# Softmax division of three attention stages: after two transposes, or on the features through DRAM

## The reference

```
x = x + SelfAttention0(layernorm(x))          # causal, 512 x 512 per head
x = x + CrossAttention0(layernorm(x), ctx)    # 64 context rows per sequence, no mask added
x = x + MixtureOfDepths(layernorm(x))         # top 128 tokens of each sequence are routed
x = x + SelfAttention1(layernorm(x))          # not causal, q and k rms-normed per head
x = x + CrossAttention1(layernorm(x), ctx, mask)
x = x + MixtureOfExperts(layernorm(x))        # 8 experts, top 2
attention = softmax(q @ k.T) @ v, heads side by side, then @ W_out
```

## Time and profile before

| | us |
|---|---|
| median of 3 runs | 2571.24 |
| lowest, highest | 2565.96, 2574.76 |
| the profiled execution, whole | 2568.06 |
| its span, first to last instruction | 2566.3 |
| self attention, causal | from about 63 to 512 |
| cross attention, routed | about 512 to 827 |
| self attention, normed | about 1070 to 1641 |

### The profile page before, as it was taken

How to read it: one execution, slowest core, us unless ns; L and a number is a source line. 1 busy time by engine, 2 the same in 40 slices (tenths; PEclk the granted TensorE clock), 3 DMA queues, 4 the chain that set the end, 5 groups by cost and what they waited for, 6 DMA issues and landing times. The chain is left out here.

```text
span 2566.3 us, 45589 instructions
## 1 busy us (share of the span) xinstructions
PE 2330.6 (91%) x14571; PEld 1519.5 (59%) x14585; DVE 1457.3 (57%) x3885; ACT 1140.1 (44%) x2685; POOL 734.6 (29%) x848
## 2 busy tenths in 40 slices
PE   7999999889996799899999999888886799999998
PEld 5455555545555566533443333445556599999997
DVE  4766676446765443577777767354545733444333
ACT  1666656523331562277777776422221033333332
POOL 3111111044421321333333221153311433333333
PEclk9999999999998999999999999999995899999999
DMA  6222222120000310322222121100009122222221
GB/s 156 88 87 90 87 76 88 31 76 5 5 1 1 105 44 1 93 63 72 66 76 68 58 73 53 40 7 9 9 1 362 57 36 33 36 36 36 36 35 22
DMA packets 135325, 148.85 MB, mean 58 GB/s; under 512 B 25286, under 2 KB 119152, under 8 KB 135024
## 3 DMA queue, kind: packets, MB, share of 16 engines
q1 hardware_dynamic: 119504, 127.23, 16.1%
q0 software_dynamic: 13680, 17.84, 4.3%
q10 hardware_dynamic: 1968, 1.60, 0.4%
HBM read 100.71 MB, written 46.01 MB: 57 GB/s over the span
## 5 line engine op out<-in xcount | busy, mean ns | idle before, releaser
L452 ACT ACTIVATE self_probs<-self_score_ps 128x512 f32<-128x512 f32 (+3 forms) x1024 | 481.0, 516 | 315.0 <-PE self_score_ps L813 162.7
L618 DVE TENSOR_REDUCE self_neg_max<-self_max_ps 128x1 f32<-128x512 f32 x512 | 328.2, 685 | 147.8 <-PE self_max_ps L799 143.3
L799 PE MATMUL self_max_ps<-self_k_stack,self_q_stack 96*128 96x512 bf16 (+3 forms) x1024 | 347.6, 342 | 21.1 <-DVE self_neg_max L615 12.3
L810 PE MATMUL self_score_ps<-self_q_stack,self_k_stack 99*128 99x512 bf16 (+3 forms) x1024 | 342.5, 342 | 1.6 <-ACT self_probs L452 1.6
L2259 ACT ACTIVATE x_stream<-experts_up_ps,experts_bias_now 128x128 f32<-128x128 f32 x568 | 162.4, 369 | 387.7 <-PE experts_up_ps L2480 387.7
L615 DVE CUSTOM_DVE_ANT_0 self_masked<-self_max_ps,self_later 128x128 f32<-128x128 f32 (+3 forms) x512 | 235.4, 488 | 124.1 <-PE self_max_ps L799 112.7
L2480 PEld LDWEIGHTS experts_up_ps<-experts_tileT,x_stream 128*128 128x128 f32 x2272 | 266.7, 193 | 5.3 <-issue 1.8
L2480 PE MATMUL experts_up_ps<-experts_tileT,x_stream 128*128 128x128 f32 x2272 | 267.2, 276 | 1.4 <-DVE x_stream L2396 1.4
L2490 PE MATMUL experts_down_ps<-experts_down,x_stream 128*128 x1136 | 256.8, 379 | 0.0
L824 PE MATMUL self_out_ps<-self_probs,self_values 128*32 128x512 f32 (+3 forms) x2048 | 231.8, 524 | 3.3 <-ACT self_probs L452 1.4
L810 PEld LDWEIGHTS self_score_ps<-self_q_stack,self_k_stack 99*128 99x128 bf16 x1024 | 98.8, 97 | 229.1 <-ACT self_probs L452 171.2
(11 more groups left out here) (293 smaller groups left out, 3962.7 us busy)
## 6 DMA issues: line engine op xcount, KB each, us to landing
self_parts_dram<-self_parts SPq DMA_DIRECT2D x64, 384.0 KB, 2.3
self_q_stack<-self_parts_dram SPq DMA_DIRECT2D x384, 64.0 KB, 2.3
self_k_stack<-self_parts_dram SPq DMA_DIRECT2D x360, 64.0 KB, 2.3
experts_up<-moe_up_dram SPq DMA_DIRECT2D x8, 1024.0 KB, 8.3
experts_down<-moe_down_dram SPq DMA_DIRECT2D x8, 1024.0 KB, 10.6
x_stream<-x_dram SPq DMA_DIRECT2D x8, 512.0 KB, 7.8
expert_rows_dram<-experts_down SPq DMA_DIRECT2D x8, 512.0 KB
out_dram<-x_stream SPq DMA_DIRECT2D x8, 512.0 KB, 8.6
```

The source lines that it names most:

```text
L452: act.activation(probs[:, i % 8, 0:w], score_ps[:, (16 * n + i) % 3, 0:w], ACT.Exp).then_inc(exp_done, 1)
L618: dve.tensor_reduce(neg_max[:, n % 2, t, h:h + 1], max_ps[:, i % 2, 0:w], AX, ALU.max, negate=True).then_inc(max_read, 1)
L799: last = pe.matmul(max_ps[:, i % 2, 0:w], q_stack[0:ROWS, h, P * t:P * t + P], k_stack[0:ROWS, h, 0:w], start=True, stop=True)
L810: last = pe.matmul(score_ps[:, m % 3, 0:w], k_stack[0:KROWS, head, P * j:P * j + P], q_stack[0:KROWS, head, S - w:S], start=True, stop=not ...
```

## The change

The division is done on features by tokens, so nothing is turned. `out_ps` is copied as before; SyncE stores `o_raw` to DRAM, and loads it back twice when a half (8 heads) of a sequence is complete: the feature rows to `o_now`, and one sum row of each head repeated 16 times to `sums`. ScalarE takes Ln of `sums` and Exp of minus that (the reciprocal); VectorE multiplies the two. Done in both self attentions and the routed cross attention. `ot`, `ob`, the copy after `ob` and the four (self: four periods') pairs of reciprocal and product go; in the self stages the last two periods of the stage keep them. In the normed self stage (`norm`) `mt` moves from chunk 0 to chunk 1 and `copy_shift` from chunk 1 to chunk 2 (`MT_STEP`). In the routed stage the loads of the next stage's weights (`router.loads()`) are issued later on SyncE, and a load of the context is issued up to three sequences ahead. The masked cross attention has the old text, in a function of its own; the routed one is a new function.

The core of the diff, self attention first:

```diff
+        out_scratch = nc.dram_tensor(f"{name}_out_dram", [2, 2 * GH, 2, HD, S], F32).ap()
+        MT_STEP = 1 if norm else 0
-            if j == 0 and n + 1 < N:
+            if j == MT_STEP and n + 1 < N:
                 work.append(("mt", n + 1))
-            if j == 1 and n >= 1:
+            if j == 1 and n == N - 1:
                 work.append(("ot", n - 1))
-                work += {(1, 1): [("ob", b - 1, 1)], (2, 0): [("e", b - 1, 0)], (2, 1): [("e", b - 1, 1)]}.get((g, j), [])
+                work += {(2, 0): [("e", b - 1, 0)], (2, 1): [("e", b - 1, 1)]}.get((g, j), [])
-            if (g, j) == (3, 1):
-                work.append(("ob", b, 0))
+                def out_store(n):
+                    b, g = n // NG, n % NG
+                    sp.wait_ge(o_copied, n + 1)
+                    wait(sp, out_loaded[g // 2], 32 * b)
+                    sp.dma_start(out_scratch[g // 2, GH * (g % 2):GH * (g % 2) + GH].rearrange("h c d t -> (h c d) t"),
+                                 o_raw[:, n % 2]).then_inc(out_stored[n % 2], 16)
+                def out_load(b, half):
+                    for i in range(2):
+                        sp.wait_ge(out_stored[i], 16 * (2 * b + half) + 16)
+                    wait(sp, o_done, 2 * (b - 1) + half + 1 if b else 0)
+                    sp.dma_start(o_now[:, half], out_scratch[half, :, 0]).then_inc(out_loaded[half], 16)
+                    sp.dma_start(sums[:, half], out_scratch[half, :, 1, 0:1].to_broadcast([2 * GH, HD, S])).then_inc(out_loaded[half], 16)
                 for b in range(B):
                     more = b + 1 < B
+                    if b >= 1:
+                        out_store(4 * b - 1)
                     place_shift(4 * b + 1)
+                    if b >= 1:
+                        out_load(b - 1, 1)
                     if more:
                         store(b + 1, 0)
                         stack(b + 1, 0)
+                    out_store(4 * b)
                     place_shift(4 * b + 2)
                     if more:
                         store(b + 1, 1)
                         stack(b + 1, 1)
+                    out_store(4 * b + 1)
                     place_shift(4 * b + 3)
+                    out_load(b, 0)
                     if more:
                         stack(b + 1, 2)
+                        out_store(4 * b + 2)
                         place_shift(4 * b + 4)
                         stack(b + 1, 3)
-                def turned_back(b, k):
+                def inverted(b, half):
+                    act.wait_ge(out_loaded[half], 32 * b + 32)
+                    act.activation(sums[:, half], sums[:, half], ACT.Ln).then_inc(sums_logged, 1)
+                    act.wait_ge(sums_logged, 2 * b + half + 1)
+                    act.activation(sums[:, half], sums[:, half], ACT.Exp, scale=-1.0).then_inc(sums_inverted, 1)
-                        if j == 1 and n + 1 < N:
+                        if j == MT_STEP + 1 and n + 1 < N:
                             copy_shift(n + 1)
                         if (g, j) == (1, 2) and b >= 1:
-                            turned_back(b - 1, 1)
+                            inverted(b - 1, 1)
-                        if (g, j) == (3, 2):
-                            turned_back(b, 0)
+                        if (g, j) == (3, 0):
+                            inverted(b, 0)
+                def normalise(b, half):
+                    dve.wait_ge(sums_inverted, 2 * b + half + 1)
+                    wait(dve, e_full, 2 * b)
+                    dve.tensor_tensor(oT[:, half], o_now[:, half], sums[:, half], ALU.mult).then_inc(o_done, 1)
-                        if j == 2 and n >= 1:
-                            normalise(n - 1)
+                        if (g, j) == (3, 2):
+                            normalise(b, 0)
+                        if (g, j) == (1, 3) and b >= 1:
+                            normalise(b - 1, 1)
```

The routed cross attention, steps and SyncE:

```diff
             steps = [("S", b, 0)]
-            steps += [("ob", b - 1, 0)] * last + [("M", b + 1, 0)] * more + [("xt", b + 2, 0)] * next2
+            steps += [("M", b + 1, 0)] * more + [("xt", b + 2, 0)] * next2
             steps += [("PV", b - 1, 1)] * last + [("xt", b + 2, 1)] * next2
             steps += [("S", b, 1)]
-            steps += [("ot", b - 1, 2)] * last + [("M", b + 1, 1)] * more + [("sr", b - 2, 0)] * choice
-            steps += [("ot", b - 1, 3)] * last + [("q", b + 2, 0)] * next2
+            steps += [("M", b + 1, 1)] * more + [("sr", b - 2, 0)] * choice
+            steps += [("q", b + 2, 0)] * next2
             steps += [("S", b, 2)]
-            steps += [("q", b + 2, 1)] * next2 + [("M", b + 1, 2)] * more + [("ob", b - 1, 1)] * last + [("PV", b, 0)]
+            steps += [("q", b + 2, 1)] * next2 + [("M", b + 1, 2)] * more + [("PV", b, 0)]
             steps += [("e", b - 1, 0)] * last
             steps += [("S", b, 3)]
-            steps += [("ot", b, 0)] + [("M", b + 1, 3)] * more + [("bk", b - 2, 0)] * choice + [("e", b - 1, 1)] * last
-            steps += [("ch", b - 2, 0)] * choice + [("ot", b, 1)] + [("v", b + 1, 0)] * more
+            steps += [("M", b + 1, 3)] * more + [("bk", b - 2, 0)] * choice + [("e", b - 1, 1)] * last
+            steps += [("ch", b - 2, 0)] * choice + [("v", b + 1, 0)] * more
+                def out_load(b, half):
+                    sp.wait_ge(out_stored[half], 16 * b + 16)
+                    wait(sp, e_full, 2 * b)
+                for b in range(B):
+                    if b >= 1:
+                        out_store(b - 1, 1)
+                        out_load(b - 1, 1)
+                    out_store(b, 0)
+                    out_load(b, 0)
+                    if b + 3 < B:
+                        load(b + 3)
```

More of the change, by code:

```diff
@@ L1047, in shift @@
                     least = neg_max[:, b % 2, :, 8 * half:8 * half + 8].unsqueeze(3).to_broadcast([P, TT, 8, S2])
-                    if masked:
-                        own = mask_in[:, b % 2].unsqueeze(2).to_broadcast([P, TT, 8, S2])
-                        pool.tensor_tensor(shifts[:, half], least, own, ALU.add).then_inc(shifted, 1)
-                    else:
-                        pool.tensor_copy(shifts[:, half], least).then_inc(shifted, 1)
+                    own = mask_in[:, b % 2].unsqueeze(2).to_broadcast([P, TT, 8, S2])
+                    pool.tensor_tensor(shifts[:, half], least, own, ALU.add).then_inc(shifted, 1)
                 def add_bias(b):
@@ L1178, in _ @@
                     exponentials(b, 1)
-                    if routed and b >= 2:
-                        scores_copied(b - 2)
                     if next2:
@@ new lines, in _ @@
+                statistics(1)
+                layer_norm(1)
+                statistics(2)
+                dve.wait_ge(ready, 1)
+                dve.wait_ge(rest_loaded, 16 * 4)
+                valued(0)
+                maxima(0, 0)
+                maxima(0, 1)
+                layer_norm(2)
+                maxima(0, 2)
+                maxima(0, 3)
+                for b in range(B):
+                    more, next3 = b + 1 < B, b + 3 < B
+                    if more:
+                        maxima(b + 1, 0)
+                    if more:
+                        maxima(b + 1, 1)
+                    if b >= 1:
+                        normalise(b - 1, 2)
+                        normalise(b - 1, 3)
+                    if more:
+                        maxima(b + 1, 2)
+                    if b >= 1:
+                        add(b - 1, 0)
+                    normalise(b, 0)
+                    if more:
+                        maxima(b + 1, 3)
+                    if next3:
+                        statistics(b + 3)
+                    if b >= 1:
+                        add(b - 1, 1)
+                    normalise(b, 1)
+                    if more:
+                        valued(b + 1)
+                    if next3:
+                        layer_norm(b + 3)
@@ L1368, in _ @@
                         layer_norm(b + 3)
-                if routed:
-                    route_statistics(B - 2)
-                    route_scores(B - 2)
-                normalise(B - 1, 2)
-                normalise(B - 1, 3)
-                if routed:
-                    compare(B - 2, range(TT))
-                    choose(B - 2)
+                route_statistics(B - 2)
+                route_scores(B - 2)
+                normalise(B - 1, 0)
+                compare(B - 2, range(TT))
+                choose(B - 2)
+                normalise(B - 1, 1)
                 add(B - 1, 0)
@@ L1379, in _ @@
                 dve.wait_ge(x_done, 2 * B)
-                if routed:
-                    route_statistics(B - 1)
-                    route_scores(B - 1)
-                    compare(B - 1, range(TT))
-                    choose(B - 1)
+                route_statistics(B - 1)
+                route_scores(B - 1)
+                compare(B - 1, range(TT))
+                choose(B - 1)
             @block.tensor
```

661 lines of the change are left out of this document (498 added, 163 removed).

## The result

| | us |
|---|---|
| before, median in the same comparison | 2571.59 |
| after, median | 2550.03 |
| ratio, 95% interval | 0.9916 (0.9894 to 0.9939) |
| the profiled execution after, whole (span) | 2543.23 (2541.5) |

The change brought 21.5 us, 0.8%, of the 57 forecast; the time is 1 us above the upper end of the range. The profile's head and the same kinds of stretch as in the earlier trace rows; the columns are those of the rows there.

The account below looks back on a forecast made before the run. TensorE's list was taken as the bound in both self attentions, with TensorE-VectorE handovers in the routed cross. Gains of 18 (causal), 19 (normed) and 20 (routed) sum to 57 us, from 2571.24 to 2514; 8-in-10 range 2486 to 2549.

Parts of the forecast that it names:

- A set of transposes is worth 0.44 us: TensorE: four overlapping transposes take 0.44 us; 45 sets removed give 19.8 us per self stage, 48 give 21.1 routed.
- Causal: 19.8 - 5 + 3 = 18: Causal self stage: transposes 19.8 us, less 5 for ScalarE in two chunks, plus 3 from VectorE; range 8 to 24.
- The rival of coupled engines: TensorE runs at round-trip pace; half the self stages' transpose gain and half the cross gain go: 29 us, 2542; chance 0.21.
- Normed: 19.8 + 12.6: Normed self stage: removed transposes give 19.8 us; `mt` one chunk later removes the GpSimd wait, 12.6 us.
- Late shifts - 9: Normed stage: the shift, copied a chunk later, lands after the next period's first score tile: 9 us lost, bounds 2 to 15.
- Chunk (1, 1) - 2: Normed stage: ScalarE has 3.9 us of work against TensorE's 3.2 in this chunk; 0.3 us each, 2 us lost.
- Loads - 2: Normed stage: ScalarE waits 1 to 3 us for loads, hidden by a projection except in the last two sequences: 2 us lost.
- The rule of the Trainium skill: Both loads, having 8 heads, use 8 DMA engines and land later; up to 7 us in the normed stage, giving 2521.
- Routed: 3.0 us a sequence: Routed cross attention: `q` 1.7 us earlier plus 1.3 us of transposes, six sequences; with other parts 20 us, range 6 to 27.
- without `ot` the `q` can start 1.7 us earlier: Routed stage, TensorE: projection `q` starts at 670.4 rather than 672.10, as `ot` 3 no longer waits for VectorE.
- a clock below 0.97: Routed cross attention: a granted clock falling below its 0.97 was named as showing the prediction wrong; no size given.
- Late loads: Rival of late shifts and loads: `out_load` holds SyncE, shift rows come late; at 1.5 us each 36 us slower, 2607; chance 0.07.

Follow-up runs that it names:

- late_inverse: The changed kernel with the first half's Ln and Exp moved from chunk (3, 0) to (3, 2), its product to (3, 3), in both self attentions: 2522.76 us, ratio 0.9808.
- mt_chunk0: late_inverse with the normed stage's turning of the maxima back in chunk 0 and the shift's copy back in chunk 1: 2555.74 us, ratio 0.9932.
- wide_loads: The changed kernel with the loads of `o_now` and `sums` written with 16 features, not 8 heads, as outer dimension: 2531.22 us, ratio 0.9845.
- q_before_sr: The changed kernel with late_inverse, wide_loads, causal `rest` later, `router.loads()` before the first sequence, and projection `q` ahead of `sr`: 2503.33 us, ratio 0.9743.
- spin_in_wait: The changed kernel with `router.loads()` before the routed stage's first sequence, plus 8 unread products in TensorE's wait at `sr`: 2532.99 us, ratio 0.9846.

## Why the prediction was wrong, point by point

The step under all the others was "TensorE's list is the bound there, so its removed work should come back nearly in full". Of the 57 us forecast the two profiled executions show 24.8: 14 are missing in the causal stage, 9.5 in the routed one, 7.5 in the normed one, where an oversized charge for late shifts hid a much undersized one for the loads. (The depths stage lost 1.1.) In the terms of the sum:

- **A set of transposes is worth 0.44 us**: right as a duration. Chunk (2, 1) of the causal stage, where nothing else is behind, fell from 4.71 to 4.27.
- **Causal: 19.8 - 5 + 3 = 18**. The step that failed is the charge for coupling. I counted ScalarE in chunks (0, 1) and (1, 1) and gave 3 us back for VectorE; in truth VectorE's list, with a wait for ScalarE's part ahead of two maxima, sets chunks 1 and 2 of g = 0 and g = 3. Of 2.64 us a sequence 0.95 came, 4.4 in all score tiles, as the last sequence grew by 1.1. The earlier trace rows showed only 11.2 us of waiting for VectorE and I read so small a wait as slack; that the transposes filled the rest is my reading, which fits the 0.60 that appeared without them. The rival of coupled engines is right here, and at g = 1 partly (7.20 to 6.92); its "half of the gain" was still too kind.
- **Normed: 19.8 + 12.6**: the sum held (31.9 of 32.4, by late_inverse), the split did not (1.4 and 30.5, by mt_chunk0). The turning of the maxima was no separate bonus of 12.6: with it in chunk 0 the removed transposes hardly counted.
- **Late shifts - 9**: mis-sized, 1.0 us. Of the first tiles only that of period 31 waited, with its weight load.
- **Chunk (1, 1) - 2**: 3.68 us where 4.04 - 0.88 + 0.44 gives 3.60: 0.6 us in seven sequences.
- **Loads - 2**: the term that cost the normed stage its gain, 17.7 us by late_inverse. Two errors. The landing was bounded by a store's 2.3 us and half of a large load, and took 6.7 beside the stack loads; and "with a projection of 1.7 us on TensorE behind it: hidden" did not hold: 7.7 us came through in the six sequences that have the projection, and 10.0 in the last two, where I had 2. Of these, the clock behind the wait is a part. The rule of the Trainium skill that I quoted and left out of the sum ("DMA: Bandwidth & Descriptors", Rules for kernel authors: the outer dimension sets how many engines share a transfer) is confirmed by wide_loads: a share of 8 engines, then of 15. Its price, 7 us in the prediction, was 18 for the whole kernel.
- **Routed: 3.0 us a sequence**: 2.6 where the clock did not differ (31.9 to 29.3). The step "without `ot` the `q` can start 1.7 us earlier" failed: `q` stands behind `sr`, whose wait for the scores took the time. q_before_sr shows what it needed. Against the 20 stood 10.5; 4.3 us went to the order of `router.loads()`, which I had not followed past the new store on SyncE, and 6.7 to the clock (spin_in_wait). 10.5, 4.3 and 6.7 are 21.5; that this is so near to 20 is luck in part, as the 10.5 are uncertain by the 6 us of the result. I had named a clock below 0.97 as a sign of being wrong, but given it no price.
- **The rivals**: of the forecasts, that of coupled engines (2542) came nearest, and by luck: it has 10, 9 and 10 us for the stages, the traces 4.0, 11.5 and 10.5, and what the last two lost went to the loads, to the order on SyncE and to the clock, not to coupling. Late loads were real, by another way than I had it: not SyncE's list behind them, but ScalarE in front of them.

## What to carry to other kernels

An engine that is 96% busy does not promise that removed work comes back: look at each chunk for the list that would be second, and above all for a wait of it that does not shrink. When work leaves a place, move something into the hole, and price the new wait at its clock too, since a busy TensorE that begins to wait loses more than the wait. Bound a new transfer by its rows and by how many engines its pattern lets it use, and put its reader as late as its own reader allows.

## What the runs showed of the hardware

- **Loads**: 256 rows of 2 KB took 3.5 us from first start to last end with 8 heads as the outer dimension (wide_loads: 2.4 us with 16 features), 84 ns for a row in both, at DMA shares of 0.49 and, in the middle, 0.94.
- **A queue is shared by what is ahead of it**: the same 512 KB store landed after 8.2 us behind 12 loads of weights and after 2.7 without them.
- **TensorE's clock**: waits of 1.7 to 3.6 us amid work at 2.4 GHz were followed by 3.4 us or more at 1.2 GHz in most cases, not in all (none behind one of 2.00 us at 635.4 in the changed kernel, nor behind one of 1.68 at 1323.7 in mt_chunk0), and the work in those 3.4 us then costs about 1.7 us more. Filling the wait with products, needed or not, kept the clock.
- **VectorE beside GpSimd**: in the changed kernel's chunk (1, 3) of the normed stage a product of two tiles lasts 1.46 us, elsewhere 0.68:

```profile
1513.59 1.15 POOL L355 TENSOR_TENSOR self_parts<-self_rest,self_parts 128x512 bf16<-128x512 f32 x1 [0.72 <-ACT self_parts L461]
...
1513.83 1.46 DVE L660 TENSOR_TENSOR self_oT<-self_o_now,self_sums 128x512 f32<-128x512 f32 x1
```

The excess, 0.78 us, is most of the 0.91 that GpSimd's instruction still ran. The Trainium skill ("SBUF — State Buffer", SBUF: two separate sides) says that VectorE with two operands in SBUF and GpSimd share one pair of ports, which one instruction holds until its end; the trace agrees. It cost nothing here: the chunk lasts 4.57 before and 4.62 after.
